# Causal ALiBi attention plus top-1 experts: the row-sum products of a round move from the middle of the next round's scores to directly in front of its value products

## The chip, the cores and the metric

The kernel runs on one core of a Trainium2 chip. The metric is the device time of one execution in microseconds (us), the median over several runs. "The profile" is one execution recorded by the hardware profiler; its times are us from the first instruction.

## What is computed

The input x is 2 x 2048 x 512 in float32. The kernel normalises each row and adds causal attention (16 heads of 32, ALiBi bias) and one expert of eight to the residual:

```python
x = L0_attn_x
xn = _layernorm(x, axis=-1)
x = x + _L0_attn_ref(xn, W_qkv, W_o) + _L0_ffn_ref(xn, wg, W, b)

# inside _L0_attn_ref
attn = jnp.einsum('bhqd,bhkd->bhqk', q, k) / math.sqrt(HEAD_DIM)
attn = attn + alibi_bias(seq_len, N_HEADS)[None] + causal_mask(seq_len)[None, None]
attn = jax.nn.softmax(attn, axis=-1)
y = jnp.einsum('bhqk,bhkd->bhqd', attn, v)
```

The change touches only how the softmax's denominators (the row sums of the exponentials) are accumulated.

## The kernel before, in words

Four parts follow one another: `project_and_route` (q, k, v and the router), `attend`, `run_experts`, and `combine`. The change lies in `attend`, from about 360 to 1668 us.

**Groups and rounds.** `attend` works through 8 groups (0 to 7) of four heads. Groups 2 to 5 are two passes of a hardware loop over two groups; the others are written out. A group has 40 rounds, numbered r = 0 to 39, in `ROUNDS`. A round is one block of 128 keys against one chunk of up to 512 queries. There are four query chunks: rounds 0 to 3, 4 to 11, 12 to 23 and 24 to 39. The last four rounds of each chunk are on the diagonal and cover 512, 384, 256 and 128 queries; the other 24 are full.

**Engines in a round.** TensorE computes four score products (one per head, line 1126; on the diagonal a small mask product, line 1129, follows each). ScalarE takes the exponentials (line 1061) out of a ring of three score banks. Between the scores TensorE also computes products for a later chunk or the next group whose row maxima VectorE takes (lines 1091, 1094, 975), from a ring of three banks. After the scores of round r, TensorE multiplies the exponentials of round r - 1 with the values (line 1170), four products of 32 output rows each. GpSimd adds the exponentials of two full rounds together (`pair_sum`, line 959), so that one product with a block of ones gives the row sums of both.

**Row sums.** `row_sums` computes the denominators: four products of 32 rows with ones, from `pair_sum` (`pair_product`, line 1137) two rounds after the pair's last, and from the exponentials themselves in a diagonal round (line 1161). In 24 rounds of a group (r = 1 to 4, 8 to 12, 16, 18, 20 to 24, 28, 30, 32, 34, 36 to 39) the step of TensorE holds such a group of products; it stands after the third score. After the last round both kinds already stand next to each other.

**Chunk ends.** ScalarE copies both accumulators out (`leave`, line 1043) after the exponentials of rounds 0, 4, 12 and 24. That copy waits for the last value products of the chunk, and for the store of the buffer that it writes (`y_stored`, line 851). VectorE then takes reciprocals (line 1010), GpSimd multiplies (line 936), and the SP queue stores.

**The maxima's way back.** `PLAN_MID` (and `PLAN_FIRST`, `PLAN_LAST`) say in which round which maxima are scored. A TURN event (line 1114) transposes the folded maxima of a chunk; ScalarE and VectorE split them (`max_hi` line 1035, `max_lo` line 993) and SP loads them into `q_aug` (`max_rows`, lines 842, 846). In `PLAN_MID` the TURNs stand in rounds 14, 18, 26 and 38. On the SP queue the 9 MB of the next group (`load_qk`, lines 813 to 817, and v, line 834) are issued behind the max_rows that follow the TURN of round 38, and the store of the chunk that the previous group ended with is issued behind these.

The loop on TensorE that sets the order of a round:

```python
for hh in range(HG):
    if r < NR:
        score_unit(half, r, hh, first, exps)
    if r and hh == HG // 2 and has_row_sums(r - 1):
        row_sums(g, r - 1, exps, adds)
    maxima(events[len(events) * hh // HG:len(events) * (hh + 1) // HG], banks, g, half, taken)
if r:
    value_products(g, half, r - 1, exps)
```

Of the kernel before, what the change touches and what calls it, by code (L numbers as in the profile page):

```python
# [26 lines left out]
HG = P // DH  # L27
# [109 lines left out]
def plan_of(g, last):  # L137

    if last:
        return PLAN_LAST, BANKS_LAST  # L140
    if isinstance(g, int) and g == 0:
        return PLAN_FIRST, BANKS_FIRST
    return PLAN_MID, BANKS_MID
# [597 lines left out]
def attend(nc, m):  # L741
# [6 lines left out]
    with ExitStack() as c:  # L748
# [48 lines left out]
        def base(eng, g, per_group):  # L797

            if isinstance(g, int):
                return g * per_group  # L800
            r = eng.alloc_register(f"base{nc.next_id()}")
            eng.reg_mov(r, g * per_group)
            return eng.snap(r, min_val=2 * per_group, max_val=G * per_group)

        with nc.Block() as block:
# [268 lines left out]
            def _(pe):  # L1074
# [41 lines left out]
                def score_unit(half, r, hh, first, exps):  # L1116

                    cc, jb = ROUNDS[r]
                    off = max(0, jb - TPC * cc) * P
                    diag = jb >= TPC * cc  # L1120
                    u = r * HG + hh
                    back, e = earlier_user(u, S_BANKS, NSU)
                    if not (first and back):

                        pe.wait_ge(exp_done, exps + (e + 1 - back * NSU))
                    last = nc.tensor.matmul(score_ps[:, u % S_BANKS, off:CH], k_aug[0:ROWS, half, hh, jb * P:(jb + 1) * P],  # L1126
                                            q_aug[0:ROWS, half, hh, cc * CH + off:(cc + 1) * CH], start=True, stop=not diag)
                    if diag:
                        last = nc.tensor.matmul(score_ps[:, u % S_BANKS, off:off + P], m.ident_bf[:], m.mask_kq[:],  # L1129
                                                start=False, stop=True)  # L1130
                    last.then_inc(scored, 1)

                def pair_product(p, start, adds):

                    for hh in range(HG):
                        pe.wait_ge(pair_added, adds + (p * HG + hh + 1))
                        last = nc.tensor.matmul(den_ps[hh * DH:(hh + 1) * DH, :], m.ones[:], pair_sum[:, p % 2, hh],  # L1137
                                                start=start, stop=False)
                    last.then_inc(pair_used, 1)

                def probs_of(g, r, exps):
                    cc, jb = ROUNDS[r]
                    if jb == 0:

                        wait_past(pe, accs_left, g * QC + cc)
                    pe.wait_ge(exp_done, exps + (r + 1) * HG)

                def has_row_sums(r):
                    return r not in PAIR_OF or r - 2 in PAIR_LAST.values()

                def row_sums(g, r, exps, adds):

                    cc, jb = ROUNDS[r]
                    off = max(0, jb - TPC * cc) * P
                    probs_of(g, r, exps)

                    if r - 2 in PAIR_LAST.values():
                        pair_product(PAIR_OF[r - 2], ROUNDS[r - 2] == (cc, 1), adds)
                    if r not in PAIR_OF:
                        for hh in range(HG):  # L1160
                            nc.tensor.matmul(den_ps[hh * DH:(hh + 1) * DH, off:CH], m.ones[:],  # L1161
                                             probs[:, r % P_SLOTS, hh, off:CH], start=jb == 0, stop=r == LAST_ROUND[cc])

                def value_products(g, half, r, exps):
                    cc, jb = ROUNDS[r]
                    off = max(0, jb - TPC * cc) * P
                    if not has_row_sums(r):
                        probs_of(g, r, exps)
                    for hh in range(HG):
                        last = nc.tensor.matmul(y_ps[hh * DH:(hh + 1) * DH, off:CH],  # L1170
                                                v_sb[:, half, jb, hh * DH:(hh + 1) * DH],
                                                probs[:, r % P_SLOTS, hh, off:CH], start=jb == 0, stop=r == LAST_ROUND[cc])
                    last.then_inc(pv_done, 1)

                def step(g, half, first, last):
                    if first:
                        pe.wait_ge(first_loaded[2], AUG)
                    pe.wait_ge(v_loaded[half], 16 * (g // 2 + 1))
                    exps, adds = base(pe, g, NSU), base(pe, g, NPAIR * HG)
                    taken = base(pe, g, NMU), None if last else base(pe, g + 1, NMU)  # L1180
                    plan, banks = plan_of(g, last)
                    for r in range(NR + 1):
                        events = [e for e in plan[r] if e[1] in (UNIT, TURN)] if r < NR else []
                        if r < NR and ROUNDS[r][1] == 0:

                            cc = ROUNDS[r][0]
                            pe.wait_ge(max_rows_loaded[cc % 2], MAX_ROWS * (g * (QC // 2) + cc // 2 + 1))
                        for hh in range(HG):
                            if r < NR:
                                score_unit(half, r, hh, first, exps)  # L1190
                            if r and hh == HG // 2 and has_row_sums(r - 1):
                                row_sums(g, r - 1, exps, adds)
                            maxima(events[len(events) * hh // HG:len(events) * (hh + 1) // HG], banks, g, half, taken)
                        if r:
                            value_products(g, half, r - 1, exps)

                pe.wait_ge(first_loaded[0], AUG)
                events = [e for e in PLAN_BEFORE[0] if e[1] in (UNIT, TURN)]
                maxima(events, BANKS_BEFORE, 0, 0, (0, None))
                groups(pe, step)  # L1200


# [313 lines left out]
```

## Time and profile before

| | |
|---|---|
| three runs | 1939.15 us median (1935.37 to 1945.24) |
| span of the profiled execution | 1937.1 us; the page gives no other time for it |
| TensorE matmul busy | 1789.7 us (92%) |
| VectorE busy | 1131.4 us (58%) |
| ScalarE busy | 913.7 us (47%) |
| GpSimd busy | 665.3 us (34%) |

Engines are named PE (TensorE), PEld (its weight loads), DVE (VectorE), ACT (ScalarE), POOL (GpSimd) and SPq (the SP queue). In a timeline a matmul's record includes its way through the array, so consecutive records overlap; the price of an instruction in a stream is the distance from its start to the next start. A float32 product of 32 rows is two instructions, so four products are shown as one record "x8". Some matmul records are missing in the trace, so an "x4" or "x3" is not always all of a step.

### The profile page before, as it was taken

Reading aid. Unit: us, or ns where it says so; the run is one execution under the profiler, and the core shown is the slowest. Engines: PE = TensorE matmul, PEld = TensorE weight load, DVE = VectorE, ACT = ScalarE, POOL = GpSimd, SP = SyncE. Lnnn points to the kernel's source line nnn. Section 1 sums busy time; section 2 is a strip of 40 time slices with the busy share of each in tenths; the row PEclk is TensorE's granted clock in tenths of the full one; section 3 lists DMA queues with packets and bytes.
Section 4 is the critical chain, followed back from the end, with each engine's and each line's share of the span. In section 5 each row is a group of like instructions: output and inputs, shape, how many; then the busy total and the mean of one; then the engine's idle time right before and its main releaser. Section 6 shows DMA issues by size and latency. Waiting matters only on the chain. (4 is left out here: it accounts for less than half of the span.)

```text
span 1937.1 us, 31890 instructions
## 1 busy us (share of the span) xinstructions
PE 1789.7 (92%) x10482; PEld 1023.6 (53%) x10483; DVE 1131.4 (58%) x2001; ACT 913.7 (47%) x1575; POOL 665.3 (34%) x665
## 2 busy tenths in 40 slices
PE   5999999589699999999999999999999999789798
PEld 4777777344344444444444444444444443478687
DVE  5433334577487577666665667767766670344366
ACT  3222222055356566565565566656656567621211
POOL 6000000067152452442444246245244346211260
PEclk9999999588899899999899899999989999899999
DMA  6667744959508205502700900730450230244496
GB/s 229 220 216 261 266 168 147 163 204 252 64 7 145 32 7 104 68 14 58 114 8 9 169 8 7 139 39 7 99 72 8 76 116 12 104 152 163 145 390 240
DMA packets 102350, 227.81 MB, mean 118 GB/s; under 512 B 9832, under 2 KB 27240, under 8 KB 96648
## 3 DMA queue, kind: packets, MB, share of 16 engines
q1 hardware_dynamic: 87648, 176.20, 36.3%
q0 software_dynamic: 14560, 49.75, 7.0%
q8 instruction: 84, 1.38, 0.3%
q14 instruction: 58, 0.48, 0.1%
HBM read 128.47 MB, written 96.93 MB: 116 GB/s over the span
## 5 line engine op out<-in xcount | busy, mean ns | idle before, releaser
L1061 ACT ACTIVATE probs_sb<-score_ps,bias 128x512 f32<-128x512 f32 (+3 forms) x1280 | 733.1, 624 | 506.2 <-PE score_ps L1129 303.7
L975 DVE TENSOR_REDUCE part_max<-max_ps 128x1 f32<-128x512 f32 (+3 forms) x1280 | 722.0, 603 | 394.5 <-PE max_ps L1091 203.0
L959 POOL TENSOR_TENSOR pair_sum<-probs_sb 128x512 f32<-128x512 f32 x384 | 479.8, 1281 | 592.5 <-ACT probs_sb L1061 592.3
L1126 PE MATMUL score_ps<-q_aug,k_aug 100*128 100x512 f32 (+3 forms) x1280 | 531.1, 422 | 42.3 <-ACT probs_sb L1061 24.4
L1091 PE MATMUL max_ps<-k_aug,q_aug 98*128 98x512 f32 (+3 forms) x1280 | 523.6, 421 | 40.1 <-DMA q_aug<-q_rows_d 33.4
L1126 PEld LDWEIGHTS score_ps<-q_aug,k_aug 100*128 100x128 f32 x1280 | 251.3, 197 | 305.9 <-ACT probs_sb L1061 231.5
L1091 PEld LDWEIGHTS max_ps<-k_aug,q_aug 98*128 98x128 f32 x1280 | 260.2, 204 | 181.7 <-DVE part_max L975 104.7
L1170 PE MATMUL acc_ps<-probs_sb,v_sb 128*32 128x512 f32 (+3 forms) x2560 | 308.6, 555 | 0.0
L1010 DVE RECIPROCAL acc_sb<-acc_sb 128x128 f32<-128x128 f32 x128 | 119.6, 939 | 74.0 <-ACT acc_sb L1043 74.0
L618 DVE SCALAR_TENSOR_TENSOR st_lo<-group_ps,st_hi 128x512 fp32r<-128x512 f32 x64 | 44.3, 692 | 139.1 <-ACT st_hi L665 138.4
L1094 PE MATMUL max_ps<-mask_qk,ident_bf 128*128 128x128 bf16 x512 | 124.3, 243 | 0.0
L1129 PE MATMUL score_ps<-mask_kq,ident_bf 128*128 128x128 bf16 x512 | 120.0, 235 | 0.0
L665 ACT ACTIVATE st_hi<-group_ps 128x512 fp32r<-128x512 f32 x64 | 38.3, 598 | 143.0 <-PE group_ps L728 124.2
L728 PE MATMUL group_ps<-xT_hi,w_hi 128*128 128x512 f32 x256 | 102.7, 401 | 0.0
L1137 PE MATMUL acc_ps<-pair_sum,ones 128*32 128x512 f32 x768 | 102.3, 605 | 0.0
L728 PE MATMUL group_ps<-xT_lo,w_hi 128*128 128x512 f32 x256 | 101.9, 398 | 0.0
L728 PE MATMUL group_ps<-xT_hi,w_lo 128*128 128x512 f32 x256 | 101.7, 397 | 0.0
L1161 PE MATMUL acc_ps<-probs_sb,ones 128*32 128x512 f32 (+3 forms) x1024 | 97.3, 452 | 1.2 <-ACT acc_sb L1043 1.2
L1094 PEld LDWEIGHTS max_ps<-mask_qk,ident_bf 128*128 128x128 bf16 x512 | 52.7, 103 | 75.1 <-issue 56.9
L1129 PEld LDWEIGHTS score_ps<-mask_kq,ident_bf 128*128 128x128 bf16 x512 | 50.6, 99 | 69.1 <-issue 48.6
L1170 PEld LDWEIGHTS acc_ps<-probs_sb,v_sb 128*32 128x32 f32 x2560 | 51.5, 109 | 63.7 <-issue 39.8
L466 POOL DMA_DIRECT2D slot_x_d<-zero_f x20 | 14.2, 715 | 172.2 <-PE group_ps L728 172.2
(177 smaller groups left out, 1684.5 us busy)
## 6 DMA issues: line engine op xcount, KB each, us to landing
k_aug<-k_hi_d SPq DMA_DIRECT2D x14, 1024.0 KB
q_aug<-q_hi_d SPq DMA_DIRECT2D x14, 1024.0 KB
slot_x_d<-zero_f POOLq DMA_DIRECT2D x20, 512.0 KB, 7.1
rows<-slot_x_d SPq DMA_DIRECT2D x40, 256.0 KB, 2.6
slot_y_d<-y_rows POOLq DMA_DIRECT2D x39, 256.0 KB, 2.5
xn_d<-xn SPq DMA_DIRECT2D x8, 1024.0 KB, 9.9
q_hi_d<-st_hi SPq DMA_DIRECT2D x32, 256.0 KB, 7.7
q_lo_d<-st_lo SPq DMA_DIRECT2D x32, 256.0 KB, 7.6
```

The costliest lines, as they stand in the source:

```text
L728: last = nc.tensor.matmul(group_ps[:, n % BANKS], lhs, rhs, start=(k == 0 and p == 0), stop=(k == KC - 1 and p == 2))
L959: nc.gpsimd.tensor_tensor(pair_sum[:, p % 2, hh], probs[:, s0, hh], probs[:, s1, hh], ALU.add).then_inc(pair_added, 1)
L975: nc.vector.tensor_reduce(part_max[:, hh * QT + i, kc:kc + 1], max_ps[:, bank, 0:w], AX.X, ALU.max).then_inc(max_taken, 1)
L1010: nc.vector.reciprocal(quarter, quarter).then_inc(inverted, 1)
L1061: nc.scalar.activation(probs[:, r % P_SLOTS, hh, off:CH], score_ps[:, (r * HG + hh) % S_BANKS, off:CH], ACT.Exp, bias=bias[:, half, hh * Q ...
L1091: last = nc.tensor.matmul(max_ps[:, bank, 0:w], q_aug[0:ROW_MAX, half, hh, i * P:(i + 1) * P], k_aug[0:ROW_MAX, half, hh, kc * CH:kc * CH ...
L1094: last = nc.tensor.matmul(max_ps[:, bank, w - P:w], m.ident_bf[:], m.mask_qk[:], start=False, stop=True)
L1126: last = nc.tensor.matmul(score_ps[:, u % S_BANKS, off:CH], k_aug[0:ROWS, half, hh, jb * P:(jb + 1) * P], q_aug[0:ROWS, half, hh, cc * CH ...
L1129: last = nc.tensor.matmul(score_ps[:, u % S_BANKS, off:off + P], m.ident_bf[:], m.mask_kq[:], start=False, stop=True)
L1137: last = nc.tensor.matmul(den_ps[hh * DH:(hh + 1) * DH, :], m.ones[:], pair_sum[:, p % 2, hh], start=start, stop=False)
L1161: nc.tensor.matmul(den_ps[hh * DH:(hh + 1) * DH, off:CH], m.ones[:], probs[:, r % P_SLOTS, hh, off:CH], start=jb == 0, stop=r == LAST_ROUN ...
L1170: last = nc.tensor.matmul(y_ps[hh * DH:(hh + 1) * DH, off:CH], v_sb[:, half, jb, hh * DH:(hh + 1) * DH], probs[:, r % P_SLOTS, hh, off:CH] ...
```

## The change

`row_sums` is called after all scores and maxima of the round, directly in front of `value_products`. Nothing else differs: the instructions are the same, and only TensorE's order moves. A TURN that stood behind the row sums of its round now stands ahead of them.

```diff
@@ -1188,10 +1188,10 @@
                         for hh in range(HG):
                             if r < NR:
                                 score_unit(half, r, hh, first, exps)
-                            if r and hh == HG // 2 and has_row_sums(r - 1):
-                                row_sums(g, r - 1, exps, adds)
                             maxima(events[len(events) * hh // HG:len(events) * (hh + 1) // HG], banks, g, half, taken)
                         if r:
+                            if has_row_sums(r - 1):
+                                row_sums(g, r - 1, exps, adds)
                             value_products(g, half, r - 1, exps)
```

The first place is TensorE's order in round 20 of group 1, the first diagonal round of the third chunk. Before:

```order
L1126 MATMUL score_ps<-q_aug,k_aug 128x512
L1129 MATMUL score_ps<-mask_kq,ident_bf 128x128
L1137 MATMUL acc_ps<-pair_sum,ones 32x512 x4
L1091 MATMUL max_ps<-k_aug,q_aug 128x512
L1126 MATMUL score_ps<-q_aug,k_aug 128x512
L1129 MATMUL score_ps<-mask_kq,ident_bf 128x128
L1091 MATMUL max_ps<-k_aug,q_aug 128x512
L1170 MATMUL acc_ps<-probs_sb,v_sb 32x512 x4
```

These are the third and fourth scores of the round with their masks, and the row sums between them. In the change the row sums stand behind the last maximum product, and the two groups of 32-row products touch, as they do in every one of the 24 rounds.

The second place is the end of round 38 of group 1, again on TensorE, with the TURN (line 1114). Before:

```order
L1137 MATMUL acc_ps<-pair_sum,ones 32x512 x4
L1161 MATMUL acc_ps<-probs_sb,ones 32x384 x4
L1091 MATMUL max_ps<-k_aug,q_aug 128x512
L1126 MATMUL score_ps<-q_aug,k_aug 128x256
L1129 MATMUL score_ps<-mask_kq,ident_bf 128x128
L1091 MATMUL max_ps<-k_aug,q_aug 128x512
L1114 MATMUL max_ps<-ident,neg_max 128x128
L1170 MATMUL acc_ps<-probs_sb,v_sb 32x384 x4
```

And now:

```order
L1091 MATMUL max_ps<-k_aug,q_aug 128x512
L1126 MATMUL score_ps<-q_aug,k_aug 128x256
L1129 MATMUL score_ps<-mask_kq,ident_bf 128x128
L1091 MATMUL max_ps<-k_aug,q_aug 128x512
L1114 MATMUL max_ps<-ident,neg_max 128x128
L1137 MATMUL acc_ps<-pair_sum,ones 32x512 x4
L1161 MATMUL acc_ps<-probs_sb,ones 32x384 x4
L1170 MATMUL acc_ps<-probs_sb,v_sb 32x384 x4
```

Both kinds of row sums of that round moved behind the TURN.

## Rows read from the trace of the kernel before

**Rows 1.** The page: busy time of each engine over the span

```profile
PE 1789.7 (92%) x10482; PEld 1023.6 (53%) x10483; DVE 1131.4 (58%) x2001; ACT 913.7 (47%) x1575; POOL 665.3 (34%) x665
```

**Rows 2.** Timeline, TensorE, round 6 of group 3, without row sums (start, us)

```profile
923.75 0.50 PE L1126 MATMUL score_ps<-q_aug,k_aug 100*128 100x512 f32 x1
...
925.26 0.40 PE L1126 MATMUL score_ps<-q_aug,k_aug 100*128 100x512 f32 x1
925.50 0.40 PE L1091 MATMUL max_ps<-k_aug,q_aug 98*128 98x512 f32 x1
```

**Rows 3.** Timeline, TensorE, round 18 of group 3: row sums of a pair

```profile
976.84 0.39 PE L1126 MATMUL score_ps<-q_aug,k_aug 100*128 100x512 f32 x1
977.16 1.07 PE L1137 MATMUL acc_ps<-pair_sum,ones 128*32 128x512 f32 x8
978.15 0.50 PE L1091 MATMUL max_ps<-k_aug,q_aug 98*128 98x512 f32 x1
978.49 0.40 PE L1126 MATMUL score_ps<-q_aug,k_aug 100*128 100x512 f32 x1
```

**Rows 4.** Timeline, TensorE, groups 2 to 3: rounds 38, 39 and the group's end

```profile
896.43 1.06 PE L1137 MATMUL acc_ps<-pair_sum,ones 128*32 128x512 f32 x8
897.31 0.83 PE L1161 MATMUL acc_ps<-probs_sb,ones 128*32 128x384 f32 x8
898.07 0.50 PE L1091 MATMUL max_ps<-k_aug,q_aug 98*128 98x512 f32 x1
...
900.45 0.23 PE L1129 MATMUL score_ps<-mask_kq,ident_bf 128*128 128x128 bf16 x1
900.49 0.48 PE L1091 MATMUL max_ps<-k_aug,q_aug 98*128 98x512 f32 x1
...
900.87 0.23 PE L1129 MATMUL score_ps<-mask_kq,ident_bf 128*128 128x128 bf16 x1
901.03 0.64 PE L1161 MATMUL acc_ps<-probs_sb,ones 128*32 128x256 f32 x8
901.60 0.50 PE L1091 MATMUL max_ps<-k_aug,q_aug 98*128 98x512 f32 x1
...
902.90 0.40 PE L1161 MATMUL acc_ps<-probs_sb,ones 128*32 128x128 f32 x8
903.12 0.40 PE L1170 MATMUL acc_ps<-probs_sb,v_sb 128*32 128x128 f32 x8
```

**Rows 5.** Timeline, all engines, group 3: exponentials of round 6, and round 13's wait

```profile
924.29 2.42 ACT L1061 ACTIVATE probs_sb<-score_ps,bias 128x512 f32<-128x512 f32 x4 [0.47 <-PE score_ps L1126]
954.48 1.02 ACT L1043 ACTIVATE acc_sb<-acc_ps 128x1024 f32<-128x1024 f32 x1 [4.13 <-DMA y_d<-acc_sb]
956.13 0.80 PE L1126 MATMUL score_ps<-q_aug,k_aug 100*128 100x512 f32 x1 [3.99 <-ACT probs_sb L1061]
```

**Rows 6.** Timeline, VectorE and the SP queue, groups 2 to 3: split, load, first store

```profile
899.81 0.27 DVE L993 TENSOR_TENSOR max_lo<-max_ps,max_hi 16x128 fp32r<-16x128 f32 x1
906.02 0.37 SPq L813 DMA_DIRECT2D k_aug<-k_hi_d  x1
...
928.59 22.79 SPq L851 DMA_DIRECT2D y_d<-acc_sb  x2
```

**Rows 7.** Timeline, ScalarE, group 4: the copy in round 12 of that group

```profile
1117.97 1.03 ACT L1043 ACTIVATE acc_sb<-acc_ps 128x1024 f32<-128x1024 f32 x1
```

**Rows 8.** Timeline, TensorE, group 7: rounds 15 and 16, without maxima

```profile
1589.97 0.96 PE L1126 MATMUL score_ps<-q_aug,k_aug 100*128 100x512 f32 x3
1591.31 0.50 PE L1126 MATMUL score_ps<-q_aug,k_aug 100*128 100x512 f32 x1 [0.38 <-ACT probs_sb L1061]
1592.74 0.96 PE L1126 MATMUL score_ps<-q_aug,k_aug 100*128 100x512 f32 x3
1596.06 0.50 PE L1126 MATMUL score_ps<-q_aug,k_aug 100*128 100x512 f32 x1
```

**Rows 9.** Timeline, TensorE, group 0: round 21 waits for group 1's load

```profile
504.67 0.47 PE L1091 MATMUL max_ps<-k_aug,q_aug 98*128 98x128 f32 x1 [15.57 <-DMA q_aug<-q_rows_d]
```

## The prediction

> **What bounds the kernel now.** The page comes first: TensorE is busy in 92% of the span, VectorE in 58%, ScalarE in 47% [rows 1]. So an order that costs TensorE less should shorten the span, unless something else sets the pace where the time is saved. I therefore went to TensorE's timeline and read distances from start to start in one group of heads.
>
> A stream of 512-column products goes at 0.24 us each (925.26 to 925.50) [rows 2]. A group of four 32-row products costs more than its own work. Going in, the distance from the last wide product is 0.32 us in place of 0.24; the group takes 0.99; and the wide product behind it takes 0.34 in place of 0.24, as its successor's start shows [rows 3]. Where two such groups touch, the first takes 0.88 (896.43 to 897.31) [rows 4]. At the group's end row sums and value products already touch as the change will have them everywhere: 128 columns take 0.22 (902.90 to 903.12) [rows 4], a quarter of 0.88, so the join itself shows no cost.
>
> The idle times come next. Per group of heads TensorE stands about 4 us in round 13, at the fourth score, for an exponential. ScalarE is behind there because its copy of the accumulators waited 4.13 us for a store [rows 5]. That store was issued at 928.59, behind the next group's 9 MB, whose issue began at 906.02 [rows 6]; the copy starts at 954.48, which is 48.5 us after the load's first issue. The trace has this stall in groups 1, 2, 3, 5 and 6. In those groups, time that TensorE saves between the load and round 13 makes the stall longer and nothing shorter.
>
> **The change part by part.** Nothing is added or removed. 24 groups of row sums per group of heads move behind the fourth score and its maxima, 192 in all; VectorE, ScalarE, GpSimd and SP keep their order.
>
> *What one move saves.* In a full round: 0.08 going in, 0.11 of the group's own 0.99, and 0.10 behind it [rows 2, 3], together 0.29; I take 0.30. In a diagonal round the row sums stand behind a mask product: 0.16 going in (900.87 to 901.03) in place of 0.04 (900.45 to 900.49) [rows 4], so 0.12, and 0.11 for the exit; what follows the mask product is slow either way. I take 0.24. Nine of the 24 rounds are full (4, 12, 16, 18, 24, 28, 30, 32, 34), 15 are diagonal.
>
> The Trainium skill (page "TensorE: Matmul & The Clock Gate", Part 3, "What overlaps and what doesn't") says that a weight load runs beside matmuls in flight only when their row groups differ. All products here use all rows, so by that rule the join would expose weight loads; its outcome is the second rival below.
>
> *Cover for the fourth score.* It now comes one group earlier. It needs the bank of the round's first score. With the round at 923.75 the first exponential runs from 924.29 and the four take 2.42, so 0.61 each: the bank is free at 924.90, and the score stood at 925.26 without a wait [rows 2, 5]. Slack 0.36 us, in a round that already has no row sums. So rounds with maxima pay nothing. After a copy (rounds 1, 5, 13, 25) ScalarE is 1.02 us later, and there part of a saving turns into a wait: I take 0.1 in place of 0.30 for rounds 4, 12 and 24, and nothing for round 1, where the copy precedes.
>
> *The TURN of round 38.* Both kinds of row sums of that round, 1.64 us (896.43 to 898.07) [rows 4], move behind it. The split that it feeds, at 899.81, comes earlier, and with it the SP queue's next load at 906.02, 6.2 us later [rows 6]. The split also waits for the round's four reductions on VectorE, so I take 1.5 us of the 1.64. The last value products of the old group, which the load needs too, still end before that.
>
> *Sum by groups of heads.* Groups 1, 2, 3, 5 and 6 go from load to load. The rounds behind the stall and up to 37 hold seven full moves (2.1, less 0.2 for round 24) and six diagonal ones (20 to 23, 36, 37: 1.4); with 1.5 from the TURN that is 4.8 each, 24.0 in all. The savings of rounds 38 to 12 vanish in the stall, which grows from 4.0 to about 4.4.
>
> Group 4 has no such stall. The loop's turn had delayed TensorE, and the copy starts at 1117.97 without waiting [rows 7]. All moves count: 0.5 for rounds 38 and 39 before it, 1.4 for six early diagonal rounds, 0.2 for rounds 4 and 12, 0.3 for round 1, 3.3 for the rest: 5.7.
>
> Group 0: round 21 waits 15.57 us for group 1's load [rows 9], which hides what comes before, except for about 0.5 by which GpSimd starts earlier. Behind it: five full moves (1.5 less 0.2) and five diagonal (1.2). Together 3.0.
>
> Group 7 has no maxima from round 15 on, so the scores come faster than the exponentials. A full round without row sums takes 2.77 (1589.97 to 1592.74) with 0.38 of waiting at the fourth score; with row sums it takes 3.32 (to 1596.06) and has no wait, because the row sums fill it [rows 8]. Now the wait stays and the sums are added: 2.77 + 0.88 = 3.65, a loss of 0.33 in each of six rounds, 2.0. Round 24 and the diagonal rounds, where the shorter exponentials are also uncovered, together lose 0.3 by the same reasoning. Against that stand 0.5 + 1.4 + 0.2 from round 38 of group 6 to round 12. Balance: 0.2 lost.
>
> Sum: 24.0 + 5.7 + 3.0 - 0.2 = 32.5 us. The profiled execution's span is 1937.1, 2 us under the median of the runs. 1939.15 - 32.5 = **1906.6; I forecast 1906 us**.
>
> Bounds of one move: below, the second rival's; above, 0.34 in a full round if the last 0.04 of the joint group's way in is saved too. That would give about 6 us more.
>
> **Rivals.**
>
> 1. *The load does not move with the TURN.* If its start hangs on the end of the old group or on something else that keeps its place, 1.5 us in each of five groups are missing: 1906 + 7.5 = 1914. For it: the old group's last value products (from 903.12, 0.22 us of work) [rows 4] end only 2.7 us before the load starts [rows 6]. Against it: that distance is more than the 1.5. Chance 0.14.
>
> 2. *The join costs.* If weights for the value products can't be loaded while the row sums run, the exit is paid as before (0.11) and a start is added (about 0.12, the diagonal entry), so each of some 121 moves that count is worth 0.24 less: 1906 + 29 = 1935. Against it: 0.22 at the group's end and 0.88 between two kinds of row sums [rows 4]. The first of these is exactly the new pair, only at 128 columns. Chance 0.07. This is the skill's rule above, against which both rows speak.
>
> 3. *Slower: the row sums were cover.* TensorE waits for the exponential at the fourth score of every full round, as it does in group 7. Each full move then loses 0.33 and each diagonal one saves nothing. Groups 1, 2, 3, 5, 6: 7 x 0.33 less 1.2 from the TURN, about 1.0 each; group 4: 9 x 0.33 = 3.0; group 0: 1.6 less 0.5; group 7: 9 x 0.33 + 0.3 = 3.3. Together about 12.5: 1952. It decides once the first exponential of a round ends over 0.36 us later than in [rows 2, 5]. The maxima between the scores speak against it. Chance 0.04.
>
> 4. *The stall in round 13 isn't tied to the load.* Then nearly all moves count in every group, 9 x 0.30 + 15 x 0.24 less 0.6 = 5.7 in each of groups 1 to 6: 34.2 + 3.0 - 0.2 = 37, 1902. Against it: copy and store [rows 5, 6]. Chance 0.03.
>
> That the change doesn't do what it says is excluded by the order of the instructions, which no scheduler touches.
>
> **How the numbers follow.** My forecast has 0.72. The range must take in the first and fourth rivals, a move worth a third more (about 1890) and one worth a third less (about 1918): **1890 to 1920**. Left out are the second and third rivals and tails of the first, under 0.2. A measurement of this kernel can tell about 0.5% (9.7 us) from no change. Faster by more: forecast, rivals 1 and 4, 0.89; within: rival 2, 0.07; slower: rival 3, 0.04.
>
> **What the profile of the change would show.** Full rounds of groups 1 to 6 with row sums get 0.3 us shorter; the row sums of a pair take 0.88 before value products, with no wait at the fourth score outside the rounds behind a copy. The distance from load to load falls by 4.8, the stall in round 13 stays at 4 to 5 us, and group 4 gains most. In group 7 full rounds with row sums take 3.6 to 3.7. I am wrong if the row sums still take 0.99 there, if waits for exponentials appear in rounds with maxima, or if the load starts no earlier, counted from the start of round 38.

## The result, and the profile after

The change runs in 1916.15 us (median of four runs, 1912.76 to 1918.73), the kernel before in 1937.34 (four runs). The two medians are 21.2 us apart; the ratio of the runs, by which I go, is 0.9871 with a 95% interval of 0.9847 to 0.9895: 25 us faster, between 20 and 30. The profiled execution's span is 1912.1 us against 1937.1, also 25.0 less. I had forecast 1906, in a range of 1890 to 1920.

The page of the changed kernel, busy times over the span and the granted clock of TensorE in 40 slices:

```profile
PE 1749.4 (91%) x10482; PEld 1042.6 (55%) x10483; DVE 1122.7 (59%) x2001; ACT 902.7 (47%) x1575; POOL 665.8 (35%) x665
PEclk9999999579799899899999899999999999899899
```

TensorE is busy 40 us less with the same 10482 matmuls [rows 1], yet the span is only 25 us shorter: the other 15 us came back as idle time of TensorE.

**What one move saves.** TensorE in round 16 of group 3 and the start of the next round:

```profile
968.14 0.23 PE L1094 MATMUL max_ps<-mask_qk,ident_bf 128*128 128x128 bf16 x1
968.30 1.06 PE L1137 MATMUL acc_ps<-pair_sum,ones 128*32 128x512 f32 x8
969.18 1.04 PE L1170 MATMUL acc_ps<-probs_sb,v_sb 128*32 128x512 f32 x8
970.15 0.50 PE L1126 MATMUL score_ps<-q_aug,k_aug 100*128 100x512 f32 x1
```

The row sums take 0.88 (968.30 to 969.18) in front of the value products, where they took 0.99 alone [rows 3]. The value products then take 0.97. Nothing is added at the join. In round 18 a TURN stands ahead of the pair:

```profile
973.67 0.50 PE L1126 MATMUL score_ps<-q_aug,k_aug 100*128 100x512 f32 x1
...
975.17 0.40 PE L1126 MATMUL score_ps<-q_aug,k_aug 100*128 100x512 f32 x1
975.41 0.40 PE L1091 MATMUL max_ps<-k_aug,q_aug 98*128 98x512 f32 x1
975.86 0.33 PE L1114 MATMUL max_ps<-ident,neg_max 128*128 128x128 f32 x1
976.11 1.24 PE L1137 MATMUL acc_ps<-pair_sum,ones 128*32 128x512 f32 x8
977.00 1.21 PE L1170 MATMUL acc_ps<-probs_sb,v_sb 128*32 128x512 f32 x8
978.14 0.50 PE L1126 MATMUL score_ps<-q_aug,k_aug 100*128 100x512 f32 x1
```

The fourth score at 975.17 follows its predecessor in the stream without a wait, as it did in [rows 2]. But the TURN comes 0.45 after the last maximum, and the round as a whole, 4.47 (973.67 to 978.14), is 0.1 longer than before (4.36). Before, the row sums stood ahead of the TURN and covered the time in which VectorE folds the maxima. This is the first sign of what I had left out.

The same round is not longer in every group. In groups 1 and 6, which are written out, round 18 takes 4.23 and 4.22 after 4.36, and round 38, the other one with a TURN and row sums, 4.67 after 4.78. In groups 2 to 5, which are in the hardware loop, they take 4.47 to 4.48 and 4.91 after the same 4.36 and 4.78, so the move loses 0.12 and 0.13 there. The value products behind such a TURN take 1.14 in the loop (977.00 to 978.14) against 0.97; why they do is not shown.

The other rounds are even in all of groups 1 to 6: a full round with row sums (16, 28, 30, 32, 34) is shorter by 0.32 to 0.33 at the mean, a diagonal one (20 to 23, 36, 37) by 0.28.

**The TURN of round 38 and the load.** TensorE, VectorE and the SP queue from group 2 to group 3, against [rows 4] and [rows 6]:

```profile
894.75 0.38 PE L1126 MATMUL score_ps<-q_aug,k_aug 100*128 100x256 f32 x1
...
896.95 0.32 PE L1114 MATMUL max_ps<-ident,neg_max 128*128 128x128 f32 x1
897.21 1.24 PE L1137 MATMUL acc_ps<-pair_sum,ones 128*32 128x512 f32 x8
898.09 1.00 PE L1161 MATMUL acc_ps<-probs_sb,ones 128*32 128x384 f32 x8
898.73 1.00 PE L1170 MATMUL acc_ps<-probs_sb,v_sb 128*32 128x384 f32 x8
```

```profile
897.93 0.27 DVE L993 TENSOR_TENSOR max_lo<-max_ps,max_hi 16x128 fp32r<-16x128 f32 x1
```

```profile
904.15 0.37 SPq L813 DMA_DIRECT2D k_aug<-k_hi_d  x1
```

In the kernel before round 38 of that group started here:

```profile
895.09 0.39 PE L1126 MATMUL score_ps<-q_aug,k_aug 100*128 100x256 f32 x1
```

From the start of round 38 (894.75) to the load it is 9.4 us; it was 10.9 (895.09 to 906.02). The split is 6.2 us ahead of the load, as in [rows 6]. The other five such loads come 1.5 or 1.6 us earlier too, but for the one at the start of group 4, which gains 1.8.

**The stall.** ScalarE and TensorE at round 13 of group 3, against [rows 5]:

```profile
952.14 1.02 ACT L1043 ACTIVATE acc_sb<-acc_ps 128x1024 f32<-128x1024 f32 x1 [4.24 <-DMA y_d<-acc_sb]
953.79 0.79 PE L1126 MATMUL score_ps<-q_aug,k_aug 100*128 100x512 f32 x1 [4.19 <-ACT probs_sb L1061]
```

The copy starts 48.0 us after the load (48.5 before). TensorE's waits there are now 4.12, 5.17, 4.19, 4.37 and 4.08 us in groups 1, 2, 3, 5 and 6, after 3.33, 3.33, 3.99, 3.98 and 3.69. Group 4 again has none.

**The last group.** Rounds 15 and 16 of group 7, without maxima, against [rows 8]:

```profile
1562.80 0.50 PE L1126 MATMUL score_ps<-q_aug,k_aug 100*128 100x512 f32 x1 [0.37 <-ACT probs_sb L1061]
1563.23 1.07 PE L1170 MATMUL acc_ps<-probs_sb,v_sb 128*32 128x512 f32 x8
1564.23 0.96 PE L1126 MATMUL score_ps<-q_aug,k_aug 100*128 100x512 f32 x3
1565.59 0.50 PE L1126 MATMUL score_ps<-q_aug,k_aug 100*128 100x512 f32 x1 [0.39 <-ACT probs_sb L1061]
1566.01 1.06 PE L1137 MATMUL acc_ps<-pair_sum,ones 128*32 128x512 f32 x8
1566.89 1.04 PE L1170 MATMUL acc_ps<-probs_sb,v_sb 128*32 128x512 f32 x8
1567.87 0.96 PE L1126 MATMUL score_ps<-q_aug,k_aug 100*128 100x512 f32 x3
```

The round with row sums keeps the wait and takes 3.64 (1564.23 to 1567.87), after 3.32.

**Group 0.** Here something stands that no row of before has. TensorE and VectorE in round 30, then the same stretch in windows of 1 us (the window and its length, busy us and instructions of PE, PEld, DVE, ACT and POOL, and then the granted clock, the DMA share and GB/s):

```profile
552.33 1.09 PE L1091 MATMUL max_ps<-k_aug,q_aug 98*128 98x512 f32 x2 [0.57 <-DVE part_max L975]
...
554.12 0.44 PE L1114 MATMUL max_ps<-ident,neg_max 128*128 128x128 f32 x1
554.49 1.94 PE L1137 MATMUL acc_ps<-pair_sum,ones 128*32 128x512 f32 x8
556.20 1.74 PE L1170 MATMUL acc_ps<-probs_sb,v_sb 128*32 128x512 f32 x8
```

```profile
551.60 3.67 DVE L975 TENSOR_REDUCE part_max<-max_ps 128x1 f32<-128x512 f32 x6
```

```profile
553.00:554.00 1.00, 1.00 (x3) 0.41 (x3) 1.00 (x3) 0.30 (x1) 1.00 (x1) 1.00 0.00 0
554.00:555.00 1.00, 0.90 (x6) 0.35 (x9) 1.00 (x3) 0.65 (x2) 0.12 (x1) 0.60 0.00 0
555.00:556.00 1.00, 1.00 (x8) 0.20 (x4) 0.46 (x2) 0.00 (x0) 0.00 (x0) 0.50 0.00 0
```

TensorE waits 0.57 us for a bank of maxima, and VectorE reduces six of them back to back, 0.61 each. Then the granted clock falls to half (1.2 instead of 2.4 GHz) from 554.2 to 557.6, and the row sums and value products take 1.71 and 1.67 instead of 0.88 and 0.97. In the kernel before the row sums stood between the third score and the maxima, and TensorE had no wait there; VectorE's row is the same length:

```profile
547.17 1.06 PE L1137 MATMUL acc_ps<-pair_sum,ones 128*32 128x512 f32 x8
548.17 0.74 PE L1091 MATMUL max_ps<-k_aug,q_aug 98*128 98x512 f32 x2
```

```profile
547.01 3.67 DVE L975 TENSOR_REDUCE part_max<-max_ps 128x1 f32<-128x512 f32 x6
```

So that round goes at VectorE's pace in both kernels, and the row sums had stood in time that TensorE had to pass anyway.

Round 16 of group 0 also has a wait that it did not have before: 2.22 us for an exponential at the fourth score, because ScalarE waited 3.66 us for GpSimd's pair sums. It lies ahead of round 21, where TensorE waits 18.45 us for the load, and so costs nothing by itself.

**Where the 25 us lie.** Each group is counted to the start of its last row sums, and in brackets stands what TensorE lost in it to the lower clock (the sum over windows of 1 us of one minus the granted clock). Group 0 is counted from the end of its wait in round 21 [rows 9], which ended at 504.67 before, 509.21 in the change and 507.71 in a second profile of it.

| us | group 0 | 1 | 2 | 3 | 4 | 5 | 6 | 7 |
|---|---|---|---|---|---|---|---|---|
| before | 84.25 (3.2) | 157.92 (5.1) | 156.06 (3.4) | 158.30 (5.1) | 160.43 (6.8) | 156.17 (3.4) | 157.94 (5.1) | 131.46 (0) |
| change | 86.28 (5.4) | 152.83 (5.1) | 154.14 (5.1) | 153.34 (5.1) | 152.72 (5.1) | 150.84 (3.4) | 149.86 (1.7) | 133.27 (1.7) |
| second profile | 83.91 (3.0) | 153.83 (5.1) | 154.00 (5.1) | 153.56 (5.1) | 154.22 (6.8) | 153.24 (5.1) | 152.88 (5.1) | 134.60 (3.4) |

Groups 1 to 6 give 33.1 us (29.7 without the 3.4 less of half clock), group 0 takes 2.0 behind its wait and 4.5 ahead of it, group 7 takes 1.8: 33.1 - 2.0 - 4.5 - 1.8 = 24.8, the difference of the spans to 0.2.

The 4.5 can be followed. SP issues group 1's load behind GpSimd's last store of x into the experts' slots (`slots_stored`): 2.7 or 2.8 us after its issue in each of the thirteen profiles of this document (457.25 to 459.99 before, 461.84 to 464.56 in the change), and the data arrive 44.3 to 45.1 us after that. 1.5 of the 4.5 us are there already when round 0 begins (392.06 before, 393.52 in the change), where the kernels do not differ. From round 0 to the arrival it takes 112.6, 112.9, 114.1 and 114.8 us in four profiles with the old order there and 112.7 to 115.8, 114.7 at the mean, in six with the new one. So at most about 1 us of it may belong to the order, and even that is within the scatter.

### The profile page after: what moved, and what is told of

It is laid out like the page before. It is cut to its first block and busy times, and to the rows that moved or that the text cites. A ratio compares the mean times of both kernels' runs of the same rounds, so it can differ in the third digit from the quotient of the medians.

```text
span 1912.1 us, 31890 instructions
## 1 busy us (share of the span) xinstructions
PE 1749.4 (91%) x10482; PEld 1042.6 (55%) x10483; DVE 1122.7 (59%) x2001; ACT 902.7 (47%) x1575; POOL 665.8 (35%) x665
## 5 line engine op out<-in xcount | busy, mean ns | idle before, releaser
L1061 ACT ACTIVATE probs_sb<-score_ps,bias 128x512 f32<-128x512 f32 (+3 forms) x1280 | 722.6, 626 | 488.5 <-PE score_ps L1129 274.9
L975 DVE TENSOR_REDUCE part_max<-max_ps 128x1 f32<-128x512 f32 (+3 forms) x1280 | 710.8, 602 | 374.9 <-PE max_ps L1091 189.2
L1091 PE MATMUL max_ps<-k_aug,q_aug 98*128 98x512 f32 (+3 forms) x1280 | 516.7, 415 | 45.1 <-DMA q_aug<-q_rows_d 36.2
L1170 PEld LDWEIGHTS acc_ps<-probs_sb,v_sb 128*32 128x32 f32 x2560 | 74.1, 111 | 105.3 <-issue 79.5
L1129 PEld LDWEIGHTS score_ps<-mask_kq,ident_bf 128*128 128x128 bf16 x512 | 50.7, 99 | 69.1 <-issue 49.3
L466 POOL DMA_DIRECT2D slot_x_d<-zero_f x20 | 14.2, 717 | 174.0 <-PE group_ps L728 174.0
```

The costliest lines, as they stand in the source:

```text
L975: nc.vector.tensor_reduce(part_max[:, hh * QT + i, kc:kc + 1], max_ps[:, bank, 0:w], AX.X, ALU.max).then_inc(max_taken, 1)
L1061: nc.scalar.activation(probs[:, r % P_SLOTS, hh, off:CH], score_ps[:, (r * HG + hh) % S_BANKS, off:CH], ACT.Exp, bias=bias[:, half, hh * Q ...
L1091: last = nc.tensor.matmul(max_ps[:, bank, 0:w], q_aug[0:ROW_MAX, half, hh, i * P:(i + 1) * P], k_aug[0:ROW_MAX, half, hh, kc * CH:kc * CH ...
```

## The experiments

Line numbers of these kernels differ by a few from those of the change. Each ratio is taken against runs of the kernel before.

**The change again, undone in the first and last group, one round of it, and the place without the join.** The edits of the last three (the fourth kernel differs from the kernel before in this line alone):

```diff
+late = not first and not (last and r > AHEAD)   # without group 0 and the end of group 7
+late = r == 38                                  # only round 38
-if r and hh == HG // 2 and has_row_sums(r - 1):
+if r and hh == HG // 2 and has_row_sums(r - 1) and not late:
     row_sums(g, r - 1, exps, adds)
...
+    if late and has_row_sums(r - 1):
+        row_sums(g, r - 1, exps, adds)
     value_products(g, half, r - 1, exps)
```

```diff
-if r and hh == HG // 2 and has_row_sums(r - 1):
+if r and hh == HG - 1 and has_row_sums(r - 1):
     row_sums(g, r - 1, exps, adds)
```

*The change, a second time.*

> The changed kernel a second time. Its first profile is 25.0 us shorter than that of the kernel before, and I had summed 32.5. By groups of heads it is 5.1, 1.9, 5.0, 7.7, 5.3 and 8.1 us shorter in groups 1 to 6, but 6.6 longer in group 0 and 1.8 longer in group 7. Theory A (the clock falls by chance): stretches at the half clock lie elsewhere this time, and group 0 and the group with 1.9 change by 1.7 us or more each, while the difference of the medians stays between 20 and 30 us. Theory B (the change makes group 0 longer: without row sums between them its five to seven maxima in a round outrun VectorE, TensorE waits, and the clock falls for a few us): group 0 is again 5 to 8 us longer than before, with waits for part_max of 0.5 us and more in rounds 9 and 26 of it and the half clock behind them.

Measured: 1915.14 us (1910.86 to 1918.95), ratio 0.9855 [0.982, 0.989]. The wait in group 0 is there again, in round 30 (the expectation counted the round wrongly), and this time without half clock:

```profile
550.07 1.10 PE L1091 MATMUL max_ps<-k_aug,q_aug 98*128 98x512 f32 x2 [0.56 <-DVE part_max L975]
...
552.12 1.06 PE L1137 MATMUL acc_ps<-pair_sum,ones 128*32 128x512 f32 x8
553.00 1.04 PE L1170 MATMUL acc_ps<-probs_sb,v_sb 128*32 128x512 f32 x8
```

So the wait belongs to the order, and the clock behind it to the execution: seven profiles in all have this wait (0.56 to 0.58 us), and only the first is followed by half clock. Neither theory holds whole: group 2, whose 1.9 the first puts down to the clock, comes out at 154.00 again, and group 0 is not 5 to 8 us longer, as the second has it. Group 0 behind round 21 takes 83.91 here, 0.3 less than before, with nearly as much half clock. The other kernels bear that out: less its half clock the stretch takes 81.0 to 81.3 us in four profiles with the old order in group 0 and 80.9 to 81.0 in five with the new one (80.9 and 81.0 in the two kernels that treat round 38 apart). So the order itself gives 0.2 to 0.3 us in group 0, where I had 2.5.

*Only round 38.*

> The kernel before, with the row sums moved in round 38 of each group alone, so that the TURN stands ahead of them there and nowhere else does anything move. My theory: the load of the next group starts 1.5 us earlier, counted from the start of round 38, and each of groups 1, 2, 3, 5 and 6 gets shorter by 1.5 + 0.24, the others by 0.24: 7 to 10 us in all, about 1929. Rival (the load does not move with the TURN, or the stall in round 13 isn't tied to the load): at most 8 x 0.24 = 2 us, 1935 or more.

Measured: 1932.3 us, ratio 0.9949 [0.9927, 0.997], that is 9.9 us faster. One moved step in each group gives a third of the whole. All loads start as early after round 38 as in the change, and the waits in round 13 shrink to 2.17, 1.95, 1.82, 3.09 and 1.71 us, because the load comes earlier and TensorE does not. The copy of group 3:

```profile
953.94 1.02 ACT L1043 ACTIVATE acc_sb<-acc_ps 128x1024 f32<-128x1024 f32 x1 [1.94 <-DMA y_d<-acc_sb]
```

It starts 48.0 us after its load at 905.97. The load moves with the TURN, and the stall with the load.

*Behind the fourth score, in front of its maxima.*

> The kernel before, with the row sums between the fourth score and the maxima behind it: one score later than before, but not touching the value products, and ahead of the TURN as before. My theory (it is the touching that saves): nothing is gained in groups 1 to 6, and group 7 loses the cover of its fourth score, 0 to 3 us: 1936 to 1941. Rival (the gain comes from the fourth score standing earlier, so that ScalarE is fed more evenly): most of the 25 us, 1925 or less.

Measured: 1946.39 us, ratio 1.0018 [0.9994, 1.0041]: no gain. The row sums of a round in which maxima follow them:

```profile
978.65 1.06 PE L1137 MATMUL acc_ps<-pair_sum,ones 128*32 128x512 f32 x8
979.65 0.50 PE L1091 MATMUL max_ps<-k_aug,q_aug 98*128 98x512 f32 x1
```

They take 1.00, where [rows 3] has 0.99. This kernel has the later place without the join, and has the waits in group 0 (0.56 in round 30, over 1.1 in round 9); the gain is the join's and the TURN's. In group 0 the later place alone costs: behind round 21, less half clock, that group takes 82.1 us, 1 us more than with the old order. In the change the join pays that back, which is why next to nothing is left of it there.

*The change without group 0 and the end of group 7.*

> The changed kernel, with group 0 and group 7 from round 15 on in the order of before. Group 7: 1.5 to 2.5 us faster than the change by both theories, since its row sums cover the fourth score again. Group 0: if the change makes it longer (theory B), it gets back the 5 to 7 us, and the kernel runs 7 to 9 us faster than the change, about 1908; if its length in the profile was chance or came from the DMAs at its start (theory A), it is 3 us slower there, and the whole is within 1.5 us of the change, about 1915.

Measured: 1913.33 us (1904.77 to 1915.59), ratio 0.9843 [0.9807, 0.9879]. The waits in group 0 are gone. The end of group 7, from round 15, takes 78.37 (before 77.23, change 81.02, second profile 82.34; of these 1.7, 0, 1.7 and 3.4 are half clock). The time of the whole can't be told from the change's: the intervals overlap over most of their length. So the waits belong to these two places; that their price is small is read from the stretches, not from the whole.

**All but round 38, and the store off the SP queue.** The first has `late = r != 38` in the edit above. In the other three GpSimd issues the store of a chunk's result right after its own multiplication, and SP issues none:

```diff
 def y_out(g, cc):
-    sp.wait_ge(y_done, g * QC + cc + 1)
-    sp.dma_start(m.y_d[g, :, cc * CH:(cc + 1) * CH], y_sb[:, cc % 2]).then_inc(y_stored[cc % 2], 16)
+    pass
...
 nc.gpsimd.tensor_tensor(y_sb[:, cc % 2], y_sb[:, cc % 2], den_sb[:, cc % 2], ALU.mult).then_inc(y_done, 1)
+pool.wait_ge(y_done, n + 1)
+pool.dma_start(m.y_d[g, :, cc * CH:(cc + 1) * CH], y_sb[:, cc % 2]).then_inc(y_stored[cc % 2], 16)
```

*All but round 38.*

> The changed kernel, with the row sums of round 38 back in the middle of the scores and so ahead of the TURN: the complement of the kernel in which only round 38 is moved. My theory (two separate gains, the touching and the earlier load): the load starts 1.5 us later again, counted from the start of round 38, and groups 1, 2, 3, 5 and 6 are 1.5 + 0.24 us longer each than in the change, 7 to 10 us in all, about 1924; the two parts add up to the change. Rival (the gains overlap, since both only feed the same stall): within 3 us of the change.

Measured: 1920.2 us, ratio 0.9904 [0.989, 0.9919], 18.6 us faster. With the 9.9 of round 38 that is 28.5; the change gives 25.0 and 28.2 in its two measurements, so the parts add up within the intervals. The loads keep their old distance, and the waits in round 13 grow to between 5.55 and 6.80 us: savings of rounds 38 to 12 do end in that stall.

*Stores by GpSimd, order of before.*

> The kernel before, with each chunk's store issued by GpSimd behind its own multiplication instead of by the SP queue behind the next group's load. My theory (the stall of round 13 hangs on the load through this store): ScalarE's copy in round 12 no longer waits, the stall of about 4 us in groups 1, 2, 3, 5 and 6 and the half clock behind it are gone, and each of these groups is 4 to 7 us shorter: 1907 to 1920. Rival (the DMA engines are simply busy with the load, whatever queue the store is in): the stall stays at over 3 us and the time within 5 us of before.

Measured: 1913.9 us, ratio 0.9882 [0.9858, 0.9906]. The copy of round 12 waits for the store of the chunk that the previous group ended with, the first of the two in this stretch. GpSimd's issue of it, and the copy, which has no wait:

```profile
921.36 0.57 POOL L937 DMA_DIRECT2D y_d<-acc_sb  x1 [0.67 <-POOL acc_sb L935]
```

```profile
942.55 1.03 ACT L1044 ACTIVATE acc_sb<-acc_ps 128x1024 f32<-128x1024 f32 x1
```

The load was still under way: its first issue is at 898.27, and its part for v, issued at 902.39, landed at 945.8. The store landed at 937.5, 16.1 us behind its issue, before the load and 5.1 us before the copy. On the SP queue the same store was issued at 928.59 [rows 6] and took 25.8 us: it landed at 954.4, 0.6 us past the load's part for v (953.8), and the copy followed at 954.48.

In groups 1, 2, 3, 5 and 6 this store takes 25.1 to 25.8 us on the SP queue and 12.1 to 16.1 from GpSimd. The load still slows it, for the stores of these groups that meet no load land in 2.4 to 2.9 us, so the rival of the expectation is half right; but it no longer ends behind the load. The medians of all 32 stores (2.7 us on the SP queue, 3.1 from GpSimd) show none of this, because most stores meet no load. The Trainium skill (page "DMA: Bandwidth & Descriptors", "Queues, rings and completion order") says that a DMA engine takes one queue's descriptors in order and turn by turn serves the queues that have work. This pair of kernels agrees: behind the load in its queue the store lands after it, from another queue before it, in 16.1 us instead of 25.8.

Groups 1, 2, 3, 5 and 6 take 151.06 at the mean after 157.28, 6.2 less, though the stall was 3.7 at the mean. The other 2.5 I put down to the clock, as TensorE's instructions and their order are the same: TensorE ran at full clock throughout these groups, where the kernel before lost 4.4 us at the mean in each. Not all of those 4.4 come back: 0.8 of them lay inside the stall, where they cost nothing, and a wait of 0.57 to 0.59 us for `part_max` in round 14 is new in each of these groups.

*Stores by GpSimd, order of the change.*

> The same with the changed kernel. My theory: with the stall gone, the moves of rounds 38 to 12 count too and the earlier TURN no longer does. Groups 1 to 6 are 5 to 6.5 us shorter each than in the kernel before with GpSimd's stores, 28 to 38 us in all; new waits for the load may appear at round 14, under 2 us a group. Rival (the change works mainly through the load's start): the distance between the two kernels shrinks to under 20 us.

Measured: 1880.56 us (1880.24 to 1882.93), ratio 0.9701 [0.9687, 0.9716], 33.3 below the same stores with the order of before. The five groups are 7.0, 5.7, 5.6, 4.9 and 7.1 shorter, 6.1 at the mean. Without the stall all of a group's moves count, near the size that I had given them: 9 x 0.30 + 15 x 0.24 - 0.6 = 5.7. That was the fourth rival's sum; its premise, that the stall has nothing to do with the load, fell with the kernels above.

*The same, with the old order in group 0 and at the end of group 7.*

> GpSimd's stores, and the changed order except in group 0 and in group 7 from round 15 on. Expected 2 to 4 us faster than the changed kernel with GpSimd's stores, since group 7 has its cover back and group 0 its spacing of the maxima.

Measured: 1880.1 us (1879.01 to 1887.16), ratio 0.9693 [0.9679, 0.9707], 0.5 below the last: not to be told apart. Group 7 from round 15 takes 77.24 against 79.77, so the uncovered fourth score costs 2.5 us there. The 2 to 4 us that I expected did not come: groups 1 and 6, where the order is the same, are 1.2 us longer each in this profile, with a wait of 0.90 for `part_max` in round 26 that the other profile lacks; why is open. The profiled execution was the slowest one; its load of group 1 arrived at 519.08 with the old order in group 0. That arrival lies at 504.7 to 507.9 in four other profiles with the old order there, and at 504.1 to 510.7 in six with the new one, so it scatters by several us with either. As above it follows GpSimd's last store into the slots, here at 471.76.

**Both products in the middle.** Behind the third score stand now the row sums and the value products together; in the first and third kernel only in group 7 from round 15 on. The first two have the stores by GpSimd, the third those of before; outside of `middle` all three have the order of the change.

```diff
+middle = last and r > AHEAD        # in the second kernel: middle = r > 0
-if r and hh == HG // 2 and has_row_sums(r - 1):
-    row_sums(g, r - 1, exps, adds)
+if middle and hh == HG // 2:
+    if has_row_sums(r - 1):
+        row_sums(g, r - 1, exps, adds)
+    value_products(g, half, r - 1, exps)
```

*Last group, stores by GpSimd.*

> GpSimd's stores and the changed order, but in group 7 from round 15 on row sums and value products stand together behind the third score. If touching and cover are two separate effects, this keeps both: the fourth score's exponential is waited for behind 1.0 to 1.9 us of products instead of in the open. A full round without row sums goes from 2.77 to about 2.45 us (ScalarE's four exponentials, 2.42, then bind), one with them from 3.65 to about 3.1. The stretch from round 15 to the end, 79.8 us in the changed kernel with GpSimd's stores, becomes 70 to 73, and the kernel 1870 to 1874. If the cover were no effect of its own, nothing changes beyond 1 us.

Measured: 1875.68 us (1874.74 to 1876.99), ratio 0.9655 [0.963, 0.9681]. The stretch takes 77.98, far from what I expected. TensorE in two rounds of it:

```profile
1529.18 0.98 PE L1127 MATMUL score_ps<-q_aug,k_aug 100*128 100x512 f32 x3
1530.47 0.50 PE L1127 MATMUL score_ps<-q_aug,k_aug 100*128 100x512 f32 x1 [0.31 <-ACT probs_sb L1062]
1530.90 1.06 PE L1171 MATMUL acc_ps<-probs_sb,v_sb 128*32 128x512 f32 x8
1531.89 0.97 PE L1127 MATMUL score_ps<-q_aug,k_aug 100*128 100x512 f32 x3
...
1533.61 1.06 PE L1138 MATMUL acc_ps<-pair_sum,ones 128*32 128x512 f32 x8
1534.49 1.04 PE L1171 MATMUL acc_ps<-probs_sb,v_sb 128*32 128x512 f32 x8
1535.46 0.73 PE L1127 MATMUL score_ps<-q_aug,k_aug 100*128 100x512 f32 x2
```

The wait of 0.31 is still there. Between two groups of products four scores still follow one another, now across the rounds' border, and with three banks the last of them waits for an exponential whatever the place. Rounds take 2.71 and 3.57 in turn, 6.28 together; the change's take 6.40. Those of the kernel before take 6.09, although it pays an exit and an entry for keeping the two groups of products apart.

*Everywhere, stores by GpSimd.*

> The same position in all groups. In rounds with maxima the fourth score has no wait that could be covered, so groups 1 to 6 should be as long as in the changed kernel with GpSimd's stores, 144 to 146 us, within 1 us each; TURNs stand behind the products again, which delays a load that nothing waits for there. So within 3 us of the kernel with only group 7 so ordered. A rival: ScalarE's copies begin half a round earlier and the waits behind them in rounds 1, 5, 13 and 25 go: up to 1 us less per group.

Measured: 1872.84 us (1870.32 to 1874.61), ratio 0.9643 [0.9619, 0.9666], 67.3 us below the kernel before and 43 below the change. It has the lowest median of all, though its interval overlaps that of the kernel with only group 7 so ordered, 2.8 us above it. The row sums still touch the value products, and both stand between the third score and the rest of the round's maxima. No wait over 0.5 us for `part_max` is left in groups 1 to 6, where the kernel with the change's order and the same stores has one or two of 0.56 to 0.82 in each. From the load at the start of group 1 to that at the start of group 6 it takes 731.4 us against 735.0.

*Last group, stores as before.*

> The changed kernel itself (stores by SP), with row sums and value products together behind the third score in group 7 from round 15 on. Only group 7 changes: its stretch from round 15 on goes from 81 to 82 us in the two profiles of the change to 70 to 73, and the kernel runs 8 to 11 us faster than the change, 1904 to 1908.

Measured: 1908.84 us (1902.69 to 1914.13), ratio 0.983 [0.9802, 0.9859]. The stretch takes 77.91, not the 70 to 73 that I expected, after 81.02 and 82.34 in the change. Less their half clock those two are 79.3 and 78.9, so 1.0 to 1.4 us come from the order and the rest from the clock; the pair with GpSimd's stores, without half clock, gives 1.8 (79.77 to 77.98). The whole lies about 7 us under the change's two medians, more than this stretch accounts for; the intervals of the ratios overlap.

## Why the prediction was right, and where not

**The price of one move: right.** 0.88 in place of 0.99, no cost at the join, and in groups 1 to 6 no new wait at the fourth score outside the rounds behind a copy. A full move gave 0.32 to 0.33 for my 0.30 and a diagonal one 0.28 for my 0.24; against that, rounds 18 and 38 gave 0.13 and 0.11 in groups 1 and 6 and lost 0.12 and 0.13 in the loop. Corrected for the clock, groups 1, 2, 3, 5 and 6 are shorter by 5.1, 3.6, 5.0, 5.3 and 4.7, 4.7 at the mean (4.5 in the second profile; 5.1 and 4.9 if half clock inside the stall is not counted), for a forecast of 4.8; group 4 by 6.0 for 5.7. That the sum met so well is in part luck, since moves that gave more and rounds with a TURN that gave less cancel. The second rival (the join costs) falls with the 0.88. The trace does not agree with the rule on weight loads of the Trainium skill (page "TensorE: Matmul & The Clock Gate", Part 3, "What overlaps and what doesn't"), by which a load runs beside matmuls in flight only when their row groups differ: row sums and value products both use all rows, and the second group starts 0.88 after the first (968.30 to 969.18) with no exposed load.

**The TURN of round 38: right.** 1.5 us, in every group; the first rival falls with the kernel that moves only this round. I had 7.5 us for it in five groups, and about 2 more for the moved row sums themselves; together they gave 9.9 with an interval of 5.8 to 14.2.

**The stall tied to the load: right.** Load to copy takes 47.7 to 49.3 us in every profile with SP's stores and a stall, the waits grow when only the other rounds move, and they go once the store leaves the queue. The waits grew by 0.7 at the mean (3.66 to 4.39), where I had said 0.4.

**Group 7: right, but for the clock.** I had 3.65 for a full round with row sums; it is 3.64. The uncovered score costs 2.5 for my 2.3. The balance came out at -1.8 and -3.1 instead of -0.2: 1.7 and 3.4 of that is half clock, which I had not counted, and without it -0.1 and +0.3 are left. That half clock is not the change's work: it begins in round 25, at the end of a wait of 1.0 us that the kernel before has as well (0.99 at 1622.57), there followed by full clock.

**Group 0: the step that failed.** "Together 3.0", 2.5 of it behind round 21, rested on the sentence that rounds with maxima pay nothing. I had taken the slack from round 6 of group 3, with four maxima, and looked only at the exponentials. In group 0 the plan puts five or six maxima into a round, and a TURN into some. Where six of full width meet a TURN, as in round 30, VectorE, at 0.61 us each and without a gap, sets the pace, and row sums in mid-round were TensorE's cover. Moved behind the maxima they come on top. By the second profile round 30 takes 6.14 after 5.23, rounds 28 and 34, with five and six maxima of full width, lose too (5.01 after 4.85, 5.00 after 4.72), round 36 saves only 0.06, and only a few save what I had given them (22: 5.06 after 5.34; 23: 3.64 after 3.92; 37: 5.14 after 5.38). In all 0.2 to 0.3 instead of 2.5. It is the third rival's mechanism with another engine: VectorE's reductions, not ScalarE's exponentials. The same kind of wait at a TURN eats part of the saving in round 18 of groups 1 and 6 and, with the longer value products, all of it in groups 2 to 5.

My signs of being wrong named waits for exponentials in rounds with maxima. One came, in round 16 of group 0, in five of the six profiles with the new order there (1.13 to 3.61 us), but the wait for the load behind it covers it.

**What no step had.** Half clock: 2.3 us more of it in group 0 behind round 21 and 1.7 in group 7, 3.4 less in groups 1 to 6, in this one execution. And the arrival of group 1's load, 4.5 us later in the change's profile: it follows GpSimd's stores into the slots, scatters by several us with either order, and whether up to 1 us of it is the change's stays open.

By the sum: 32.5 forecast, 3.4 more in groups 1 to 6 from the clock, 9.5 less in group 0 (its 3.0 and the 6.5 lost), 1.6 less in group 7, which makes 24.8. A miss of 7.5 us by the spans, or 0.4%; the 4.5 us of the late arrival in it are of a size by which executions differ.

## What to carry to other kernels

Before moving work out of a stretch, ask of every engine what that work covered there: a slack read in one round holds for that round's mix, and the busiest round of the partner engine (here six reductions in a row) decides. Put narrow products next to each other, and where a wait for another engine follows, in front of it. And when several micro-savings end in one wait, look at what ends the wait: moving the small stores off the queue with the big load gave 23 us (1.2%), nearly as much as the reordering, and let the reordering give its full 33. To judge such a store, read the one that the wait hangs on, not the median of all.

## What the runs showed of the hardware

Short waits are sometimes followed by half clock, which costs more than they last. In the change's profile TensorE waited 1.25 us before 436.88 and 0.57 us before 552.33, both times with work on either side, and each time 3.4 us at half clock followed, in which it lost 1.7 us. The same waits in the second profile (1.21 and 0.56) were followed by full clock. Over all profiles half clock follows the wait of 0.56 to 0.58 once in seven times, that of 1.1 to 1.3 three times in seven, and that of 1.0 in round 25 of group 7 four times in ten. Half clock begins inside or right behind the stall of 3.3 to 5.2 us in every one of the fifteen groups that have one in the profile of before and the two of the change, and 1.7 to 5.1 us per group are lost to it; taking the stall away was worth 6.2 us per group for 3.7 us of waiting.

Float32 products with 32 output rows in a chain take 0.22 us per 128 columns and group of four (0.88 at 512, 0.22 at 128), with ones as with the values. What costs is the change between them and products with 128 output rows: about 0.1 going in, 0.1 at the exit and 0.1 on the first wide product behind them.

A 256 KB store issued behind a 9 MB load on the same queue took 25.1 to 25.8 us to land, ending with the load; issued from GpSimd beside the load it took 12.1 to 16.1 us, and without a load beside it 2.4 to 2.9.
